# Attention: the first addition of each block's sum of probabilities moves to VectorE, and one tile's sum from TensorE to GpSimd

## Chip, cores, metric

One core of a Trainium2 chip runs the whole program. The metric is the device time of one execution in microseconds; the time before is the median of three runs.

## What is computed

A transformer layer with a scale and an offset from a condition, then a second layer of running averages. Only the attention of the first layer matters here:

```python
q = h @ wq / jnp.sqrt(jnp.asarray(d, h.dtype))      # 16 heads of 32, b = 2, l = 2048
...
q = rotary_pos_emb(q)
k = rotary_pos_emb(k)
logits = jnp.einsum('bhik,bhjk->bhij', q, k)
a = jax.nn.softmax(logits, axis=-1)
y = jnp.einsum('bhij,bhjv->bhiv', a, v)
```

The softmax is taken apart: `exp(logit - max)` for each query and key, the sum of these over the keys (`l` in the kernel), and the product with `v` that is divided by the sum later on.

## The kernel before

The attention stage works through 8 units (4 groups of 4 heads, 2 sequences), each of 4 blocks of 512 queries, each block of 16 steps. A step is one tile `k` of 128 keys for the 4 heads of the group. `attend` writes out, engine by engine, what is done in each of the 512 steps; an engine takes its instructions in that order, and semaphores tie the engines together.

- **TensorE** (lines 811 to 830): for each head a score matmul (L735, keys by queries, into one of three PSUM tiles `sT`) and, for a block 19 steps ahead, a matmul for the maxima (L763, into one of three PSUM tiles `mx`). Then the product of the step before with `v` (L787). Where the tile of the step before is in `PE_SUMS` (8 and 14), matmuls with a matrix of ones add its probabilities over the keys (L798). At step 5 of the next block (`LAST_AT`) one more such sum, over `acc`, ends the block's sum (L806).
- **VectorE**: `maxima` reduces each `mx` tile (L845); TensorE may fill an `mx` tile again when its reduction is done. Twice per 16 steps there is a small extra operation (L851, L860).
- **ScalarE**: `exps` takes the exponential of each score tile (L891) into `probs`, a ring of `PR` = 8 tiles of 4 heads x 512 queries. A tile of the ring is written again 8 steps later, and only when whoever sums it has read it (`added`, `summed`). Once per block it copies the finished values (L898, `o_sb`) and the finished sum (L904, `l_sb`).
- **GpSimd**: `add_pair` issues a DMA that adds tile `k` + 1 onto tile `k` for `k` in `PAIRS` (L924). `add_round` adds one tile, or one such pair, onto `acc` (`prob_sums`), head by head, four additions per round (L942). `POOL_ROUNDS` lists for each round the step at which it is issued, counted from the block's start, and the tile it reads: (18, 12) is the pair 12 and 13, added in step 2 of the next block. The first round starts `acc` from tile 2 (`POOL_FIRST`) and pair 0 (tiles 0 and 1).
- **SyncE** loads the next unit's keys, values and queries during a unit and stores the results.

So of the 16 tiles TensorE sums two (8 and 14), and the other 14 go through `acc`: ten in pairs by DMA, and tiles 2, 5, 11 and 15 directly. The last block of the stage has lists of its own (`LAST_SUMS`, `LAST_ROUNDS`). The maxima are made by `AHEAD` = 19 steps earlier than their use, so the last 19 steps of the stage have none.

Of the kernel before, what the change touches and what calls it, by code (L numbers as in the profile page):

```python
# [9 lines left out]
ALU = mybir.AluOpType  # L10
# [6 lines left out]
G = P // KD  # L17
# [5 lines left out]
TT = TB // P  # L23
# [10 lines left out]
PR = 8  # L34
PE_SUMS = (8, 14)
PAIRS = (0, 3, 6, 9, 12)
POOL_FIRST = 2
POOL_ROUNDS = ((5, 0), (7, 5), (9, 3), (11, 6), (12, 11), (14, 9), (16, 15), (18, 12))
# [5 lines left out]
LAST_AT = 5  # L44
# [528 lines left out]
def attend(nc, c, a, s, t, ps):  # L573
# [25 lines left out]
    def added(w, h):  # L599


        k = w % LT - (w % LT - 1 in PAIRS)
        r = 0 if k == POOL_FIRST else [x for _, x in POOL_ROUNDS].index(k)
        return w // LT * POOL_ADDS + G * r + h + 1
# [13 lines left out]
    with nc.Block() as block:  # L618
# [106 lines left out]
        def _(pe):  # L725
# [65 lines left out]
            def sums(w):  # L791

                n, k = w // LT, w % LT
                if k == PE_SUMS[0] and n:
                    pe.wait_ge(s["l_kept"], n)
                pe.wait_ge(s["exp"], G * (w + 1))
                for h in range(G):
                    mm = nc.tensor.matmul(l_ps[h * KD:(h + 1) * KD, :], c["ones"][:, 0:KD], t["p"][:, w % PR, h, :],  # L798
                                          start=(k == PE_SUMS[0]), stop=False)
                mm.then_inc(s["psum"], 1)  # L800
# [35 lines left out]
        def _(dve):  # L836
# [25 lines left out]

            for at, st in enumerate(steps):
                for i in range(TT if st["job"] else 0):
                    maxima(st, i)
# [12 lines left out]
        def _(act):  # L878
            def exps(at, heads):
                for h in heads:  # L880
                    if at >= PR:

                        v = at - PR
                        if not by_pe(v):
                            act.wait_ge(s["acc_done"], added(v, h))
                        elif h == 0:
                            act.wait_ge(s["psum"], summed(v))
                        if h == 0:
                            act.wait_ge(s["pv"], v + 1)
# [26 lines left out]
        def _(pool):  # L916
# [9 lines left out]
            def add_round(n, r):  # L926
# [5 lines left out]
                for h in range(G):  # L932
                    pool.wait_ge(s["exp"], w * G + h + 1)
                    x = t["acc"][:, n % 2, h, :]
                    if r == 0:
                        if n >= 2:
                            pool.wait_ge(s["sum_done"], n - 1)
                        first = t["p"][:, POOL_FIRST % PR, h, :]
                    else:
                        pool.wait_ge(s["acc_done"], n * POOL_ADDS + G * (r - 1) + h + 1)  # L940
                        first = x
                    nc.gpsimd.tensor_tensor(x, first, t["p"][:, w % PR, h, :], ALU.add).then_inc(s["acc_done"], 1)  # L942
# [16 lines left out]
def attention(nc, c, a, t):  # L959

    with ExitStack() as ctx:
        def sb(name, shape, dt=F32):
# [8 lines left out]
                 "score exp pv psum acc_done paired0 paired1 l_in recip rl_stored sum_done o_kept l_kept y_stored l_stored "  # L971
# [1015 lines left out]
```

## Time and profile before

| what | value |
|---|---|
| median of three runs | 3648.7 us (3648.08 to 3656.93) |
| the profiled execution: its time | 3653.45 us |
| the profiled execution: its span | 3651.7 us |
| granted TensorE clock, mean over the span | 0.973 |
| attention stage within the span | 396 to 2098 us |
| TensorE, VectorE, ScalarE, GpSimd busy | 95%, 56%, 41%, 57% |

The span is the time from the first to the last instruction in the trace, and all stretches below are counted from its start. "Busy" of an engine is the time in which an instruction ran on it. A granted clock of 1.00 is 2.4 GHz. Neighbouring instructions of one engine overlap a little in the records, so the distance between starts is shorter than a duration. In a timeline, instructions of one kind that follow each other are merged into a row with their number (x4); the bracket at the end says how long the engine was idle before, and what ended it. GpSimd is called POOL there, VectorE DVE, ScalarE ACT, TensorE PE, and its weight loads PEld.

### The profile page before, as it was taken

What the parts mean: (1) busy time and instruction counts of PE and PEld (TensorE: products, weight loads), DVE (VectorE), ACT (ScalarE), POOL (GpSimd) and SP (SyncE); (2) the same over time, 40 slices, a digit from 0 to 9 for tenths busy, and PEclk for the clock granted to TensorE, in tenths of its full rate; (3) what the DMA queues carried; (4) which work ended last, traced back from release to release, by engine and by line L of the source; (5) the groups of instructions that cost most, each with busy time, mean ns of one, the idle gap of its engine ahead of it and who ended that gap; (6) DMA issues with size and microseconds to landing.
All of it is one profiled execution on the core that took longest, in us unless ns stands there. A gap on an engine that the chain in (4) does not pass through costs nothing. (4 is left out here: it accounts for less than half of the span.)

```text
span 3651.7 us, 47181 instructions
## 1 busy us (share of the span) xinstructions
PE 3451.7 (95%) x16672; PEld 2252.2 (62%) x16672; DVE 2051.3 (56%) x3299; ACT 1515.4 (41%) x2791; POOL 2095.9 (57%) x1663
## 2 busy tenths in 40 slices
PE   7999899999999999999999969999999986999997
PEld 5777445454554545455455348888888864777776
DVE  5776677777777777777777244222222213444443
ACT  2332366666666666666666622111111112211121
POOL 3654388887878888798888712222222213545453
PEclk9999899999999999999999979999999997999999
DMA  4555676868677786877765543222222114212221
GB/s 170 183 172 196 119 145 126 154 132 146 132 139 151 127 145 131 153 140 132 151 128 107 105 149 97 65 63 74 74 71 68 57 41 143 80 59 82 75 75 38
DMA packets 176739, 419.34 MB, mean 115 GB/s; under 512 B 15382, under 2 KB 62998, under 8 KB 151670
## 3 DMA queue, kind: packets, MB, share of 16 engines
q1 hardware_dynamic: 153606, 249.59, 25.9%
q0 software_dynamic: 22896, 166.73, 23.7%
q8 instruction: 132, 2.16, 0.3%
q14 instruction: 105, 0.86, 0.1%
HBM read 162.25 MB, written 87.03 MB: 68 GB/s over the span
## 5 line engine op out<-in xcount | busy, mean ns | idle before, releaser
L845 DVE TENSOR_REDUCE part_max<-ps_att 128x1 f32<-128x512 f32 x1972 | 1227.9, 684 | 400.3 <-PE ps_att L763 399.9
L891 ACT ACTIVATE probs<-ps_att 128x512 f32<-128x512 f32 x2048 | 1062.4, 602 | 545.1 <-PE ps_att L735 469.8
L942 POOL TENSOR_TENSOR prob_sums<-prob_sums,probs 128x512 f32<-128x512 f32 x884 | 1146.9, 1562 | 61.8 <-DMA probs<-probs 61.8
L787 PE MATMUL ps_att<-probs,v_tok 128*32 128x512 f32 x4096 | 550.7, 610 | 0.0
L1433 POOL TENSOR_TENSOR ff_g_lo<-ff_g,ff_g_hi 128x512 fp32r<-128x512 f32 x128 | 165.1, 1290 | 551.6 <-DVE ff_g_hi L1394 551.6
L735 PE MATMUL ps_att<-q_stack,k_first 97*128 97x512 f32 x768 | 328.0, 427 | 14.1 <-ACT probs L891 14.0
L735 PE MATMUL ps_att<-q_stack,k_stack 97*128 97x512 f32 x768 | 321.4, 427 | 10.6 <-ACT probs L891 10.0
L1302 ACT ACTIVATE ff_g<-ps_ff 128x512 f32<-128x512 f32 x128 | 76.8, 600 | 579.6 <-PE ps_ff L1186 579.6
L763 PE MATMUL ps_att<-k_first,q_stack 96*128 96x512 f32 x756 | 304.6, 403 | 7.3 <-DMA q_stack<-qk 7.3
L763 PE MATMUL ps_att<-k_stack,q_stack 96*128 96x512 f32 x768 | 303.7, 395 | 0.0
L735 PEld LDWEIGHTS ps_att<-q_stack,k_first 97*128 97x128 f32 x768 | 146.5, 191 | 199.4 <-ACT probs L891 141.3
L735 PEld LDWEIGHTS ps_att<-q_stack,k_stack 97*128 97x128 f32 x768 | 143.7, 189 | 199.1 <-ACT probs L891 146.6
L924 POOL DMA_DIRECT2D probs<-probs x159 | 152.3, 958 | 178.1 <-PE ps_att L787 161.8
L1876 POOL TENSOR_TENSOR av_gated_lo<-av_full,av_gated_hi 128x512 fp32r<-128x512 f32 x64 | 93.3, 1457 | 267.3 <-ACT av_gated_hi L1729 267.3
L1394 DVE CAST ff_g_hi<-ff_g 128x512 fp32r<-128x512 f32 x128 | 55.8, 436 | 299.6 <-ACT ff_g L1302 299.6
L942 POOL TENSOR_TENSOR prob_sums<-probs 128x512 f32<-128x512 f32 x128 | 165.1, 1434 | 52.6 <-DMA probs<-probs 50.0
L787 PEld LDWEIGHTS ps_att<-probs,v_tok 128*32 128x32 f32 x4096 | 80.9, 108 | 184.0 <-ACT probs L891 174.4
L553 POOL TENSOR_TENSOR rotated<-rot_a,rot_b 128x512 f32<-128x512 f32 x64 | 89.8, 1403 | 153.9 <-DVE rot_b L394 150.2
L763 PEld LDWEIGHTS ps_att<-k_first,q_stack 96*128 96x128 f32 x756 | 146.3, 194 | 34.3 <-DMA q_stack<-qk 7.8
L763 PEld LDWEIGHTS ps_att<-k_stack,q_stack 96*128 96x128 f32 x768 | 145.7, 190 | 26.3
L1729 ACT ACTIVATE av_gated_hi<-av_full 128x512 fp32r<-128x512 f32 x64 | 40.6, 634 | 262.8 <-DVE av_full L1837 262.8
L1186 PE MATMUL ps_ff<-ff_h_hi,w_hi 128*128 128x512 f32 x512 | 143.3, 402 | 0.7 <-ACT ff_h_hi L1314 0.7
(202 smaller groups left out, 5705.0 us busy)
## 6 DMA issues: line engine op xcount, KB each, us to landing
probs<-probs POOLq DMA_DIRECT2D x159, 1024.0 KB, 8.7
q_stack<-qk SPq DMA_DIRECT2D x144, 128.0 KB, 7.2
qk<-rot_hi SPq DMA_DIRECT2D x64, 256.0 KB, 6.5
qk<-rot_lo SPq DMA_DIRECT2D x64, 256.0 KB, 2.4
av_gate_rows<-gate SPq DMA_DIRECT2D x64, 256.0 KB
k_stack<-qk SPq DMA_DIRECT2D x24, 512.0 KB, 11.0
k_first<-qk SPq DMA_DIRECT2D x18, 512.0 KB, 10.8
x_in_sb<-in_x SPq DMA_DIRECT2D x8, 1024.0 KB, 6.7
```

The costliest lines, as they stand in the source:

```text
L553: nc.gpsimd.tensor_tensor(rot[:, u % 2, :], ra[:, u % 2, :], rb[:, u % 2, :], ALU.add)\
L735: nc.tensor.matmul(sT[u % 3], kS[b][0:S3 + 1, h, k * P:(k + 1) * P], q_rows(n)[0:S3 + 1, h, :], start=True, stop=True)\
L763: nc.tensor.matmul(mx[mx_uses % 3], q_rows(n)[0:S3, h, q * P:(q + 1) * P], kS[b][0:S3, h, k * TB:(k + 1) * TB], start=True, stop=True).the ...
L787: mm = nc.tensor.matmul(o_ps[rows, :], t["v"][:, steps[w]["b"], k, rows], t["p"][:, w % PR, h, :], start=(k == 0), stop=(k == LT - 1))
L845: nc.vector.tensor_reduce(t["pm"][:, r, k:k + 1], mx[mx_uses % 3], AX.X, ALU.max)\
L891: nc.scalar.activation(t["p"][:, at % PR, h, :], sT[(at * G + h) % 3], ACT.Exp)\
L924: nc.gpsimd.dma_start(t["p"][:, w % PR], t["p"][:, (w + 1) % PR], accum_op=ALU.add).then_inc(sem, 16)
L942: nc.gpsimd.tensor_tensor(x, first, t["p"][:, w % PR, h, :], ALU.add).then_inc(s["acc_done"], 1)
L1186: mm = nc.tensor.matmul(ps[:, 4 + u % 2, :], w[:, f, m * P:(m + 1) * P], h[:, f, :], start=(i == 0 and f == 0), stop=(i == 2 and f == DC - 1))
L1302: nc.scalar.activation(gf[:], ps[:, 4 + u % 2, :], ACT.Gelu_apprx_tanh).then_inc(s["g"], 1)
L1433: nc.gpsimd.tensor_tensor(gl[:, u % 2, :], gf[:], gh[:, u % 2, :].bitcast(F32), ALU.subtract)\
L1876: nc.gpsimd.tensor_tensor(al[:, v % 2, :], af[:, v % 2, :], ah[:, v % 2, :].bitcast(F32), ALU.subtract).then_inc(s["a_lo"], 1)
```

## The change

`PE_SUMS` becomes (8,), so TensorE sums tile 8 alone. VectorE begins each block's sum: `begin_sum` adds tile 2 to pair 0 for one head and writes `acc`, and `DVE_AT` puts the four heads into steps 6 and 7, in each behind the maxima 1 and 3 of the four. A semaphore of its own, `acc_begun`, counts them; ScalarE waits for it before it overwrites tiles 0, 1 and 2, and GpSimd's first round (tile 5) before it adds. VectorE now waits for pair 0's transfer. GpSimd's first round goes, and a round for tile 14 comes at offset 20, which is step 4 of the next block. The last sum and the copy of it move two steps on (`LAST_AT` 5 to 7).

```diff
--- before.py
+++ after.py
@@ -32,16 +32,17 @@
 EPS2 = 1e-6
 EPS_ATT = 1e-30
 PR = 8
-PE_SUMS = (8, 14)
+PE_SUMS = (8,)
 PAIRS = (0, 3, 6, 9, 12)
-POOL_FIRST = 2
-POOL_ROUNDS = ((5, 0), (7, 5), (9, 3), (11, 6), (12, 11), (14, 9), (16, 15), (18, 12))
+DVE_SUMS = (0, 2)
+DVE_AT = ((6, 1, 0), (6, 3, 1), (7, 1, 2), (7, 3, 3))
+POOL_ROUNDS = ((7, 5), (9, 3), (11, 6), (12, 11), (14, 9), (16, 15), (18, 12), (20, 14))
 POOL_ADDS = G * len(POOL_ROUNDS)
 LAST_SUMS = (8, 11, 12, 13, 14, 15)
 LAST_ROUNDS = tuple(x for x in POOL_ROUNDS if x[1] not in LAST_SUMS)
 K_AT = (2, 6, 10, 14, 18, 22)
 V_AT = (26, 30)
-LAST_AT = 5
+LAST_AT = 7
 STEPS = NB * LT
 UNITS = NG * B
 JOBS = G * TT
@@ -600,8 +601,10 @@
 
 
         k = w % LT - (w % LT - 1 in PAIRS)
-        r = 0 if k == POOL_FIRST else [x for _, x in POOL_ROUNDS].index(k)
-        return w // LT * POOL_ADDS + G * r + h + 1
+        if k in DVE_SUMS:
+            return s["acc_begun"], w // LT * G + h + 1
+        r = [x for _, x in POOL_ROUNDS].index(k)
+        return s["acc_done"], w // LT * POOL_ADDS + G * r + h + 1
 
     def pair_sem(n, k):
         m = n * len(PAIRS) + PAIRS.index(k)
@@ -791,12 +794,13 @@
             def sums(w):
 
                 n, k = w // LT, w % LT
-                if k == PE_SUMS[0] and n:
+                opening = k == shares(n)[0][0]
+                if opening and n:
                     pe.wait_ge(s["l_kept"], n)
                 pe.wait_ge(s["exp"], G * (w + 1))
                 for h in range(G):
                     mm = nc.tensor.matmul(l_ps[h * KD:(h + 1) * KD, :], c["ones"][:, 0:KD], t["p"][:, w % PR, h, :],
-                                          start=(k == PE_SUMS[0]), stop=False)
+                                          start=opening, stop=False)
                 mm.then_inc(s["psum"], 1)
 
             def last_sums(n):
@@ -860,9 +864,26 @@
                 nc.vector.tensor_copy(t["mT"][:, e % 2, :], mx[mx_uses % 3][0:JOBS, 0:P]).then_inc(s["mx_free"], 1)
                 mx_uses += 1
 
+            def begin_sum(n, h):
+
+
+                first, second = DVE_SUMS
+                if h == 0:
+                    sem, value = pair_sem(n, first)
+                    dve.wait_ge(sem, value)
+                    if n >= 2:
+                        dve.wait_ge(s["sum_done"], n - 1)
+                dve.wait_ge(s["exp"], (n * LT + second) * G + h + 1)
+                nc.vector.tensor_tensor(t["acc"][:, n % 2, h, :], t["p"][:, first % PR, h, :], t["p"][:, second % PR, h, :],
+                                        ALU.add).then_inc(s["acc_begun"], 1)
+
             for at, st in enumerate(steps):
-                for i in range(TT if st["job"] else 0):
-                    maxima(st, i)
+                for i in range(TT):
+                    if st["job"]:
+                        maxima(st, i)
+                    for k, behind, h in DVE_AT:
+                        if (k, behind) == (st["k"], i):
+                            begin_sum(at // LT, h)
                 if ending is not None:
                     keep_maxima(ending)
                     ending = None
@@ -882,7 +903,8 @@
 
                         v = at - PR
                         if not by_pe(v):
-                            act.wait_ge(s["acc_done"], added(v, h))
+                            sem, value = added(v, h)
+                            act.wait_ge(sem, value)
                         elif h == 0:
                             act.wait_ge(s["psum"], summed(v))
                         if h == 0:
@@ -933,13 +955,10 @@
                     pool.wait_ge(s["exp"], w * G + h + 1)
                     x = t["acc"][:, n % 2, h, :]
                     if r == 0:
-                        if n >= 2:
-                            pool.wait_ge(s["sum_done"], n - 1)
-                        first = t["p"][:, POOL_FIRST % PR, h, :]
+                        pool.wait_ge(s["acc_begun"], n * G + h + 1)
                     else:
                         pool.wait_ge(s["acc_done"], n * POOL_ADDS + G * (r - 1) + h + 1)
-                        first = x
-                    nc.gpsimd.tensor_tensor(x, first, t["p"][:, w % PR, h, :], ALU.add).then_inc(s["acc_done"], 1)
+                    nc.gpsimd.tensor_tensor(x, x, t["p"][:, w % PR, h, :], ALU.add).then_inc(s["acc_done"], 1)
 
             nc.gpsimd.memset(t["k1"][S3:S3 + 1].bitcast(F32), 1.0).then_inc(s["ones_set"], 1)
             pool.wait_ge(s["ones_set"], 1)
@@ -968,7 +987,7 @@
             o=sb("o_sb", [P, TB]), l=sb("l_sb", [P, TB]))
         ps = ctx.enter_context(nc.psum_tensor("ps_att", [P, 8, 512], F32))
         names = ("q_in0 q_in1 q_in2 q_in3 q_first1 q_first2 v_first k_in v_in mx_full mx_free neg_max max_set0 max_set1 "
-                 "score exp pv psum acc_done paired0 paired1 l_in recip rl_stored sum_done o_kept l_kept y_stored l_stored "
+                 "score exp pv psum acc_begun acc_done paired0 paired1 l_in recip rl_stored sum_done o_kept l_kept y_stored l_stored "
                  "ones_set")
         s = phase(nc, ctx, " ".join("at_" + n for n in names.split()))
         s = {n[3:]: v for n, v in s.items()}
```

VectorE, in the attention stage, from a block's maxima on (before):

```order
L845 TENSOR_REDUCE part_max<-ps_att 128x1 x4
L860 CAST max_turned<-ps_att 16x128
L845 TENSOR_REDUCE part_max<-ps_att 128x1 x60
L851 TENSOR_REDUCE neg_max_sb<-part_max 128x16
L845 TENSOR_REDUCE part_max<-ps_att 128x1 x4
```

And in the changed kernel, the same place:

```order
L849 TENSOR_REDUCE part_max<-ps_att 128x1 x4
L864 CAST max_turned<-ps_att 16x128
L849 TENSOR_REDUCE part_max<-ps_att 128x1 x34
L877 TENSOR_TENSOR prob_sums<-probs 128x512
L849 TENSOR_REDUCE part_max<-ps_att 128x1 x2
L877 TENSOR_TENSOR prob_sums<-probs 128x512
L849 TENSOR_REDUCE part_max<-ps_att 128x1 x2
L877 TENSOR_TENSOR prob_sums<-probs 128x512
L849 TENSOR_REDUCE part_max<-ps_att 128x1 x2
L877 TENSOR_TENSOR prob_sums<-probs 128x512
L849 TENSOR_REDUCE part_max<-ps_att 128x1 x20
L855 TENSOR_REDUCE neg_max_sb<-part_max 128x16
```

The row of 60 maxima is cut open: four additions stand in it, two maxima apart.

GpSimd, from the issue of pair 0 (step 2) to that of pair 9 (step 11), before:

```order
L924 DMA probs<-probs 128x2048
L942 TENSOR_TENSOR prob_sums<-prob_sums,probs 128x512 x4
L924 DMA probs<-probs 128x2048
L942 TENSOR_TENSOR prob_sums<-probs 128x512 x4
L942 TENSOR_TENSOR prob_sums<-prob_sums,probs 128x512 x4
L924 DMA probs<-probs 128x2048
L942 TENSOR_TENSOR prob_sums<-prob_sums,probs 128x512 x4
L924 DMA probs<-probs 128x2048
```

In the changed kernel:

```order
L946 DMA probs<-probs 128x2048
L961 TENSOR_TENSOR prob_sums<-prob_sums,probs 128x512 x8
L946 DMA probs<-probs 128x2048
L961 TENSOR_TENSOR prob_sums<-prob_sums,probs 128x512 x4
L946 DMA probs<-probs 128x2048
L961 TENSOR_TENSOR prob_sums<-prob_sums,probs 128x512 x4
L946 DMA probs<-probs 128x2048
```

Between the issue of pair 0 and that of pair 3 stand eight additions instead of four, and between pair 3 and pair 6 four instead of eight.

## Rows read from the trace of the kernel before

**Rows 1.** The page: span, then each engine's busy time, share and instructions.
```profile
span 3651.7 us, 47181 instructions
...
PE 3451.7 (95%) x16672; PEld 2252.2 (62%) x16672; DVE 2051.3 (56%) x3299; ACT 1515.4 (41%) x2791; POOL 2095.9 (57%) x1663
```

**Rows 2.** Busy time by stretch, attention; columns PE, PEld, DVE, ACT, POOL, TensorE clock, DMA.
```profile
928.00:1034.00 106.00, 106.00 (x578) 53.77 (x576) 82.53 (x136) 70.12 (x136) 88.52 (x74) 1.00 0.67 130
396.00:2098.00 1702.00, 1666.45 (x8947) 832.17 (x8947) 1246.68 (x2035) 1094.97 (x2112) 1404.72 (x1172) 0.99 0.74 136
```

**Rows 3.** Groups of instructions by line: busy us, mean ns, idle before.
```profile
L845 DVE TENSOR_REDUCE part_max<-ps_att 128x1 f32<-128x512 f32 x1972 | 1227.9, 684 | 400.3 <-PE ps_att L763 399.9
L942 POOL TENSOR_TENSOR prob_sums<-prob_sums,probs 128x512 f32<-128x512 f32 x884 | 1146.9, 1562 | 61.8 <-DMA probs<-probs 61.8
...
L798 PE MATMUL ps_att<-probs,ones 128*32 128x512 f32 x544 | 71.7, 599 | 0.0
...
L1367 DVE TENSOR_TENSOR ff_zT_lo<-ff_zT,ff_zT_hi 128x512 fp32r<-128x512 f32 x32 | 22.2, 693 | 1.1
```

**Rows 4.** Timeline of TensorE, step 9 of a block (start us, us).
```profile
1027.24 0.50 PE L735 MATMUL ps_att<-q_stack,k_first 97*128 97x512 f32 x1
...
1030.23 1.04 PE L798 MATMUL ps_att<-probs,ones 128*32 128x512 f32 x8
1031.20 0.51 PE L735 MATMUL ps_att<-q_stack,k_first 97*128 97x512 f32 x1
```

**Rows 5.** Timeline of all engines, one step without sums, microsecond 1004.68 onwards.
```profile
1004.68 0.50 PE L735 MATMUL ps_att<-q_stack,k_first 97*128 97x512 f32 x1
...
1005.45 2.48 DVE L845 TENSOR_REDUCE part_max<-ps_att 128x1 f32<-128x512 f32 x4 [0.61 <-PE ps_att L763]
...
1006.22 0.19 PEld L763 LDWEIGHTS ps_att<-k_stack,q_first 96*128 96x128 f32 x1
1006.45 0.40 PE L763 MATMUL ps_att<-k_stack,q_first 96*128 96x512 f32 x1
...
1007.78 0.50 PE L735 MATMUL ps_att<-q_stack,k_first 97*128 97x512 f32 x1
```

**Rows 6.** Timeline of GpSimd, steps 2 to 5 of the same block.
```profile
1005.33 0.88 POOL L924 DMA_DIRECT2D probs<-probs  x1 [0.78 <-PE ps_att L787]
1005.94 5.29 POOL L942 TENSOR_TENSOR prob_sums<-prob_sums,probs 128x512 f32<-128x512 f32 x4
1014.63 0.88 POOL L924 DMA_DIRECT2D probs<-probs  x1 [3.40 <-PE ps_att L787]
1015.24 5.29 POOL L942 TENSOR_TENSOR prob_sums<-probs 128x512 f32<-128x512 f32 x4
```

**Rows 7.** Timeline of VectorE and GpSimd, a VectorE subtraction in the last stage.
```profile
3253.45 1.30 POOL L1876 TENSOR_TENSOR av_gated_lo<-av_full,av_gated_hi 128x512 fp32r<-128x512 f32 x1 [2.61 <-ACT av_gated_hi L1729]
...
3253.92 1.37 DVE L1737 TENSOR_TENSOR av_zT_lo<-av_zT,av_zT_hi 128x512 fp32r<-128x512 f32 x1 [1.22 <-ACT av_zT_hi L1675]
```

**Rows 8.** Timeline of ScalarE, copies of finished values; one per block.
```profile
888.55 0.60 ACT L898 ACTIVATE o_sb<-ps_att 128x512 f32<-128x512 f32 x1 [0.52 <-PE ps_att L787]
...
950.08 0.60 ACT L898 ACTIVATE o_sb<-ps_att 128x512 f32<-128x512 f32 x1 [0.52 <-PE ps_att L787]
...
1001.71 0.60 ACT L898 ACTIVATE o_sb<-ps_att 128x512 f32<-128x512 f32 x1 [0.56 <-PE ps_att L787]
```

**Rows 9.** Timeline of GpSimd (pair 0 in three blocks), then of ScalarE (first block).
```profile
432.43 4.93 POOL L942 TENSOR_TENSOR prob_sums<-probs 128x512 f32<-128x512 f32 x4 [10.52 <-DMA probs<-probs]
...
490.83 4.95 POOL L942 TENSOR_TENSOR prob_sums<-probs 128x512 f32<-128x512 f32 x4 [9.52 <-DMA probs<-probs]
...
699.53 5.01 POOL L942 TENSOR_TENSOR prob_sums<-probs 128x512 f32<-128x512 f32 x4 [3.52 <-DMA probs<-probs]
...
423.97 2.06 ACT L891 ACTIVATE probs<-ps_att 128x512 f32<-128x512 f32 x4 [1.01 <-PE ps_att L735]
...
433.72 0.60 ACT L891 ACTIVATE probs<-ps_att 128x512 f32<-128x512 f32 x1 [4.61 <-POOL prob_sums L942]
```

## The prediction

> **What bounds the kernel now.** I began with the page [rows 1]: over the whole span TensorE is busy 95% of the time and no other engine 60%. But the change touches only the attention stage, so next came the busy time by stretch. In a quiet stretch of two blocks [rows 2] TensorE is busy for all of 106 us at a granted clock of 1.00 (2.4 GHz), VectorE for 78%, ScalarE for 66% and GpSimd for 84%. Then the timelines, to see that this is a bound and not an average. A step without sums runs from one first score to the next in 3.10 us, 1004.68 to 1007.78 [rows 5]; step 9, with the sum of tile 8, takes 3.96 us, 1027.24 to 1031.20, with the sums at 1030.23 inside it [rows 4]. So a sum costs 0.86 us of TensorE time, and it goes into the period undiminished. Sixteen steps and three sums (two tiles, and the last sum over `acc`) make 16 x 3.10 + 3 x 0.86 = 52.2 us, and a quiet block takes 1001.71 - 950.08 = 51.6 us [rows 8]. TensorE sets the pace of most blocks. The exception is a block in each unit where the loads of the next unit's keys delay the pair transfers: 950.08 - 888.55 = 61.5 us is the longest [rows 8]. I count seven such blocks with 2 to 10 us each over the quiet period, some 34 us together.
>
> GpSimd does 32 additions and five DMA issues for a block. Read by the mean duration, 32 x 1.562 = 50.0 us [rows 3], it would be full. But four of them in a row take 5.29 us with the last one counted whole [rows 6], so they start (5.29 - 1.56) / 3 = 1.24 us apart: 32 x 1.24 + 5 x 0.6 = 43 us, and the 84% of [rows 2] says the same. The Trainium skill, Perfetto Trace Analysis, section GPSIMD Engine Instruction, warns that a GpSimd span is unreliable and that spacing of starts is the thing to read; the rows agree, and by the spans a sum would come out at no gain at all.
>
> **TensorE: one sum less.** The sums of tile 14 go in 31 blocks (the last keeps its own list). The group has 544 instructions, eight for a tile, so 68 tiles [rows 3], of which 31 go: 31 x 0.86 = **-26.7 us** if nothing else fills the place. The last sum moves from step 5 to step 7; it costs the same there.
>
> **GpSimd: no more and no less.** The round that began the sum goes, a round for tile 14 at offset 20 comes: 32 additions as before. The order changes, though. In step 2 it issues pair 0 (1005.33), then adds tile 12's round (1005.94), and is free until it issues pair 3 at 1014.63, after waiting 3.40 us [rows 6]. The new round of 4 x 1.24 = 5.0 us goes into this hole, and pair 3 leaves about 1.6 us later, at 1016.2 on that clock. Its reader is the round at offset 9, four steps or 12.4 us on. Tile 14's buffer is wanted by ScalarE in step 6, one step after the round's end. The last sum, now in step 7, waits for it too, but it is over by then. I cost the round at nothing; the cover is the 3.4 us hole and 8 us of slack per block. Without that cover the reader of tile 14's buffer, ScalarE, would stand for what is missing.
>
> **VectorE: four additions of 128x512.** Two go into step 6 and two into step 7, each behind the second and the fourth maximum. Their price alone is that of the subtraction of two SBUF tiles in the second stage, 0.693 us [rows 3]; in a row they start about 0.60 us apart as the maxima do, (2.48 - 0.68) / 3 [rows 5]. What is queued behind them is the maxima, and for those TensorE waits: with three PSUM tiles, the fourth maximum's matmul of a step may begin only when the first one has been reduced. Count from the first score of step 6, with the offsets of [rows 5]. The first maximum is reduced from +0.77, the fourth matmul is at +1.77 and its weights at +1.54; the reduction ends at +1.45, so the slack is between 0.09 and 0.32 us, and I take 0.15.
> Step 6: maxima at 0.77 and 1.37, addition at 1.97 (ends 2.66), maxima at 2.57 and 3.17, second addition ready at 3.77. GpSimd adds to the first head's result from about 2.74 to 4.04 (1.30 us as in [rows 7]). That collides. In [rows 7] a VectorE subtraction of two SBUF tiles that began 0.47 us into a GpSimd addition lasted 1.37 us, and ended 0.54 us after the GpSimd one. So the second addition here ends at 4.04 + 0.54 = 4.58 and not at 4.46, and step 7's first maximum begins at 4.49 where it began at 3.87: 0.62 us late. Less the slack, TensorE stands for **0.47 us** in step 7. In step 7 the same happens, but this step now has the last sum in it and gives VectorE 0.86 us to catch up: its fourth addition ends about 8.5, step 8's first maximum is ready at 3.10 + 0.47 + 3.96 + 0.77 = 8.3, late by about the slack. No second stall. With no collision the lateness is 0.50 and the stall 0.18 to 0.41; with the slack at its least and the collision it is 0.53. Over 31 blocks: 31 x 0.47 = **+14.6 us**, bounds 5.6 and 16.4.
> The rule behind this is in the Trainium skill, SBUF - State Buffer, section Who interferes with whom: a VectorE instruction with two SBUF inputs and a GpSimd instruction that reads SBUF share one pair of ports, and the second to start is blocked until the first is over. It speaks against the change, and the rows agree with it.
>
> **The wait for pair 0 moves to VectorE.** GpSimd used to wait for that transfer, in time that it had; now VectorE waits at step 6, with the maxima behind it. In quiet blocks it has landed: the round on it began at 1015.24 behind pair 3 without a wait [rows 6]. In the first two blocks it has not: GpSimd got pair 0 at 432.43 and 490.83 [rows 9]. Step 6 of the first block started its exponentials at 423.97, so the addition would be due near 425.4 and is held 7 us, and TensorE with it from step 7's second maximum. The kernel before stood there too, but in step 8, from 431 on, and only until 433.72 [rows 9], then at GpSimd's pace. The difference is about 2.5 us in the first block and 2 in the second: **+4.5 us**, bounds 0 and 9. In the seven slow blocks GpSimd is rid of a wait and issues its pairs up to 1.1 us sooner: **-1 us**, bounds 0 and -7.
>
> **The sum.** -26.7 + 14.6 + 4.5 - 1.0 = -8.6 us. The profiled execution has a span of 3651.7 and a time of 3653.45 us; the median of the three runs is 4.75 us under the latter. I set the change against the median: 3648.7 - 8.6 = **3640 us**. The bounds of the terms together give -28 to +1.
>
> **Rivals.**
> (a) The additions are hidden wholly: the slack is larger than the rows let me see, and nothing of the stall is left. For it: VectorE is idle 0.61 us in each step [rows 5], 9.8 us a block, against 2.5 us of additions. Against it: the offsets. Time: 3648.7 - 26.7 = 3622. Chance 0.17.
> (b) Slower: every VectorE addition meets a GpSimd addition just begun and takes about 1.29 us of VectorE's time. Step 6 then holds 4 x 0.60 + 2 x 1.29 = 4.98 us of VectorE's work against a period of 3.10; the lateness of 1.88 gives a stall of 1.7, and step 7 adds 1.0 more after its sum. 2.7 - 0.86 = 1.8 us a block, 57 us: 3706. It decides against the change from a stall of 0.86 on, which is a lateness of 1.0 us, one collision of full length and no more. For it: GpSimd's new round ends only 2 us before the first addition is due, and one late transfer puts it on top. Against it: GpSimd's next round waits for each of VectorE's additions, head by head, so the two engines take turns. In full it is improbable, in part less so. Chance 0.15. By the rule of the Trainium skill named above this is what follows wherever GpSimd starts first.
> (c) Pair 0 comes late for VectorE in the blocks with loads as well, 2.3 us in each of the seven: 16 us, and 3640 + 16 = 3656. For it: the first two blocks. Against it: the longest later wait of GpSimd for pair 0 was 3.52 us, until 699.53 [rows 9], and VectorE asks one step later. Chance 0.14.
> (d) TensorE is not the bound after all and GpSimd or the transfers keep the period at 51.6: no change, 3649. The undiminished 0.86 us in [rows 4] speaks against it. Chance 0.04.
> My forecast, TensorE's gain less a short stall in step 7, has the other 0.50, with a range of its own from 3632 to 3650.
>
> **How the numbers follow.** What a measurement of this kernel can tell from no change is about 0.3%, 10.9 us. Faster than 3637.8: all of (a), 0.17, and 0.21 of the forecast's 0.50: 0.38. Slower than 3659.6: 0.13 of (b) and 0.05 of (c): 0.18. Within: the rest, 0.44. For the range I leave out the far part of (b) and the edge of (a): 3621 to 3661.
>
> **What would show it.** In the profile after: the sums group at 296 instructions instead of 544; a quiet block at 51.6 - 0.4 = 51.2 us; VectorE's additions at a mean between 0.7 and 0.9 us; idle time of TensorE's weight load before the fourth maximum of step 7, put down to VectorE, some 15 us in all; step 8 without such a stall; GpSimd's additions still 1.24 us apart. A quiet block at 50.7 would prove (a), means over 1.2 us on VectorE (b), VectorE waiting for the pair transfers beyond the second block (c), an unchanged 51.6 without stalls on VectorE (d).

## The result, and the profile after

| | before | after |
|---|---|---|
| median of four runs each | 3648.4 us | 3700.4 us |
| ratio, 95% interval | | 1.0128 (1.0109 to 1.0147) |
| span of the profiled execution | 3651.7 us | 3697.7 us |
| attention: first and last copy of values | 466.6, 2096.7 us | 469.1, 2135.6 us |

The change makes the kernel 52 us slower, where the text above forecast 9 us faster and a range up to 3661. Of the 46 us between the two spans 39 lie in the attention stage, up to the last copy of values; the other 7 are in the stages behind it, which the change does not touch; from the last copy of values to the end took 1555 to 1561 us in the other kernels of this study, 1562 here. The page (the span, then busy time, share and instructions of each engine):

```profile
span 3697.7 us, 46937 instructions
...
PE 3449.1 (93%) x16424; PEld 2252.7 (61%) x16424; DVE 2141.7 (58%) x3427; ACT 1514.2 (41%) x2791; POOL 2093.3 (57%) x1659
```

The busy time by stretch; the first row has the same microseconds as the quiet stretch of before in [rows 2], but here a stop ends in it, so it is no longer a quiet one; the second is the stage, and the last three a stop that is read below:

```profile
928.00:1034.00 106.00, 103.64 (x539) 52.28 (x543) 86.22 (x141) 66.85 (x130) 88.45 (x74) 0.96 0.66 130
396.00:2150.00 1754.00, 1658.24 (x8699) 828.22 (x8699) 1341.79 (x2168) 1097.96 (x2118) 1401.88 (x1168) 0.97 0.73 133
704.00:708.00 4.00, 0.31 (x2) 0.00 (x0) 0.00 (x0) 1.05 (x2) 0.00 (x0) 0.99 1.10 145
708.00:712.00 4.00, 1.39 (x3) 1.16 (x4) 2.74 (x5) 0.07 (x1) 1.26 (x1) 0.50 1.03 205
716.00:720.00 4.00, 4.00 (x21) 2.35 (x22) 2.81 (x5) 3.02 (x6) 4.00 (x4) 1.00 0.43 86
```

The groups of instructions by line:

```profile
L961 POOL TENSOR_TENSOR prob_sums<-prob_sums,probs 128x512 f32<-128x512 f32 x1008 | 1303.8, 1594 | 214.5 <-DVE prob_sums L877 137.8 <-ACT probs L913 69.1 <-DMA probs<-probs 7.6
...
L766 PE MATMUL ps_att<-k_first,q_stack 96*128 96x512 f32 x756 | 308.2, 408 | 42.8 <-DVE part_max L849 35.3 <-DMA q_stack<-qk 7.5
...
L877 DVE TENSOR_TENSOR prob_sums<-probs 128x512 f32<-128x512 f32 x128 | 108.3, 848 | 69.8 <-DMA probs<-probs 69.8
...
L802 PE MATMUL ps_att<-probs,ones 128*32 128x512 f32 x296 | 38.5, 592 | 0.0
```

The edit did what it says. TensorE's sums are 296 instructions where they were 544 [rows 3], VectorE's additions are there at a mean of 0.85 us, GpSimd adds nearly as often as before (1008 for 884 + 128; the last block has a round less). New are the waits of TensorE's maxima matmul for VectorE (35.3 us in this group alone, where the same group had none before) and 69.8 us in which VectorE stood before its additions for the transfer of pair 0.

**A quiet block** goes as the working above has it. VectorE's timeline in steps 6 to 8:

```profile
1032.61 1.29 DVE L849 TENSOR_REDUCE part_max<-ps_att 128x1 f32<-128x512 f32 x2 [0.62 <-PE ps_att L766]
1033.82 0.68 DVE L877 TENSOR_TENSOR prob_sums<-probs 128x512 f32<-128x512 f32 x1
1034.42 1.28 DVE L849 TENSOR_REDUCE part_max<-ps_att 128x1 f32<-128x512 f32 x2
1035.62 0.87 DVE L877 TENSOR_TENSOR prob_sums<-probs 128x512 f32<-128x512 f32 x1
1036.41 1.27 DVE L849 TENSOR_REDUCE part_max<-ps_att 128x1 f32<-128x512 f32 x2
1037.61 0.84 DVE L877 TENSOR_TENSOR prob_sums<-probs 128x512 f32<-128x512 f32 x1
...
1039.57 0.85 DVE L877 TENSOR_TENSOR prob_sums<-probs 128x512 f32<-128x512 f32 x1
1040.34 2.47 DVE L849 TENSOR_REDUCE part_max<-ps_att 128x1 f32<-128x512 f32 x4
```

The first addition takes 0.68 us; the others 0.84 to 0.87, as they run into GpSimd's. TensorE in step 7 of the same block (its first score, its fourth score, its fourth maximum, then the first score of step 8):

```profile
1034.94 0.50 PE L738 MATMUL ps_att<-q_stack,k_first 97*128 97x512 f32 x1
...
1036.47 0.40 PE L738 MATMUL ps_att<-q_stack,k_first 97*128 97x512 f32 x1
1037.14 0.49 PE L766 MATMUL ps_att<-k_stack,q_first 96*128 96x512 f32 x1 [0.27 <-DVE part_max L849]
...
1039.42 0.50 PE L738 MATMUL ps_att<-q_stack,k_first 97*128 97x512 f32 x1
```

The fourth maximum's matmul has 0.27 us of idle time ahead of it, put down to VectorE, and step 7 lasts 1039.42 - 1034.94 = 4.48 us: 3.96 with the last sum, and a stop of 0.52. The reduction at 1040.34 follows on the last addition without a gap and TensorE does not wait for it. So this block loses 0.52 us of the 0.86 us (over the quiet blocks the median of step 7 is 4.51 us against 3.93 in tile14_only, which has the last sum there and no additions on VectorE: 0.58). Blocks that were 51.6 and 52.1 us are 51.5 and 51.8.

**A block with loads** does not go as worked out. VectorE in the second block of the program's second unit:

```profile
701.05 1.29 DVE L849 TENSOR_REDUCE part_max<-ps_att 128x1 f32<-128x512 f32 x2 [0.59 <-PE ps_att L766]
709.26 0.69 DVE L877 TENSOR_TENSOR prob_sums<-probs 128x512 f32<-128x512 f32 x1 [6.92 <-DMA probs<-probs]
709.87 1.28 DVE L849 TENSOR_REDUCE part_max<-ps_att 128x1 f32<-128x512 f32 x2
711.07 0.85 DVE L877 TENSOR_TENSOR prob_sums<-probs 128x512 f32<-128x512 f32 x1
```

It stood 6.92 us for the transfer of pair 0, with two maxima of step 6 and all that follows queued behind. TensorE's next maximum matmul came after that:

```profile
710.61 0.80 PE L766 MATMUL ps_att<-k_stack,q_stack 96*128 96x512 f32 x1 [6.31 <-DVE part_max L849]
```

TensorE did nothing from 704.3 to 710.6. The granted clock was 0.50 of full speed (1.2 GHz) between 708 and 712, in the stretches above; it had fallen during the stop, stayed there until after 714 and was back at 1.00 from 716 on. Two scores in between start 0.85 us apart instead of 0.47. Step 7 took 12.5 us, 8.0 more than in a quiet block, and the whole block 61.6 us where it had been 54.0. The DMA column says that the transfer engines were busy all the while (1.10 and 1.03). Pair 0 landed here 20.6 us after its issue at 688.6 (the line says count, duration of the issue, place):

```profile
L946 POOL DMA_DIRECT2D probs<-probs x1: 1012/1012/1012, 688.6 to 688.6; - x1
...
DMA to landing us min/median/max: 20.6/20.6/20.6
```

In the kernel before, the same transfer took 13.3 us:

```profile
L924 POOL DMA_DIRECT2D probs<-probs x1: 1067/1067/1067, 686.2 to 686.2; - x1
...
DMA to landing us min/median/max: 13.3/13.3/13.3
```

The copy of values, one per block, gives the length of each block. The kernels of the study are best told by it:

| kernel | median, us | ratio to before | first copy | mean of the seven second blocks of a unit | median of the other 21 |
|---|---|---|---|---|---|
| before | 3648.4 | 1 | 466.6 | 56.2 | 51.7 |
| the change | 3700.4 | 1.0128 | 469.1 | 60.5 | 51.8 |
| tile14_only | 3658.6 | 0.9996 (0.9972 to 1.0020) | 462.8 | 59.5 | 51.0 |
| vector_only | 3719.8 | 1.0169 (1.0118 to 1.0221) | 469.4 | 59.6 | 53.2 |
| begin_2_5 | 3654.3 | 1.0000 (0.9977 to 1.0024) | 466.0 | 56.2 | 51.8 |
| all_in_step7 | 3838.4 | 1.0491 (1.0445 to 1.0537) | 469.7 | 62.3 | 58.2 |
| after_loads | 3617.8 | 0.9893 (0.9870 to 0.9916) | 459.9 | 51.4 | 51.5 |
| before_loads | 3615.7 | 0.9887 (0.9866 to 0.9907) | 458.5 | 51.6 | 51.7 |
| after_two_loads | 3632.8 | 0.9945 (0.9923 to 0.9966) | 466.8 | 51.4 | 51.7 |
| tile14_loads | 3605.4 | 0.9859 (0.9840 to 0.9879) | 458.5 | 52.2 | 50.9 |
| tile14_loads_b | 3620.8 | 0.9906 (0.9882 to 0.9930) | 457.6 | 51.3 | 51.2 |
| tile14_loads_q | 3652.2 | 0.9988 (0.9976 to 0.9999) | 458.3 | 52.8 | 54.0 |

"Second block of a unit" is here the distance from the copy in the unit's second block to that in its third, in the profiled execution; the loads of the next unit's keys at steps 18 and 22 fall in it. The kernel before had medians of 3653 to 3658 us beside the experiments and not 3648.4, so the ratios count, not the differences of medians.

By the same copies the 39 us of the attention stage divide so: 2.5 before the first copy, 30.0 in the seven second blocks, 8.0 in the first blocks of the seven later units, and -1.6 in the rest. In three of those first blocks VectorE stood 1.4, 1.4 and 1.8 us for pair 0, and step 7 took 6.0, 7.6 and 8.1 us instead of 4.5: a short wait can cost more than its own length. VectorE's first addition and two of TensorE's matmuls in the second of the three:

```profile
868.22 0.69 DVE L877 TENSOR_TENSOR prob_sums<-probs 128x512 f32<-128x512 f32 x1 [1.38 <-DMA probs<-probs]
...
869.57 0.50 PE L766 MATMUL ps_att<-k_first,q_stack 96*128 96x512 f32 x1 [0.74 <-DVE part_max L849]
...
871.55 0.65 PE L766 MATMUL ps_att<-k_first,q_stack 96*128 96x512 f32 x1 [0.65 <-DVE part_max L849]
```

After these two stops of 0.7 us the granted clock was 0.50 in the stretch 872 to 874; in the first of the three blocks, from 650 to 656, it stayed at 1.00.

### The profile page after: what moved, and what is told of

It is laid out like the page before. It is cut to its first block and busy times, and to the rows that moved or that the text cites. A ratio compares the mean times of both kernels' runs of the same rounds, so it can differ in the third digit from the quotient of the medians.

```text
span 3697.7 us, 46937 instructions
## 1 busy us (share of the span) xinstructions
PE 3449.1 (93%) x16424; PEld 2252.7 (61%) x16424; DVE 2141.7 (58%) x3427; ACT 1514.2 (41%) x2791; POOL 2093.3 (57%) x1659
## 5 line engine op out<-in xcount | busy, mean ns | idle before, releaser
L961 POOL TENSOR_TENSOR prob_sums<-prob_sums,probs 128x512 f32<-128x512 f32 x1008 | 1303.8, 1594 | 214.5 <-DVE prob_sums L877 137.8
L766 PE MATMUL ps_att<-k_first,q_stack 96*128 96x512 f32 x756 | 308.2, 408 | 42.8 <-DVE part_max L849 35.3
L946 POOL DMA_DIRECT2D probs<-probs x159 | 160.3, 1008 | 117.4 <-PE ps_att L790 112.9
L877 DVE TENSOR_TENSOR prob_sums<-probs 128x512 f32<-128x512 f32 x128 | 108.3, 848 | 69.8 <-DMA probs<-probs 69.8
L1856 DVE TENSOR_TENSOR av_full<-ps_avg,av_gate_rows 128x512 f32<-128x512 f32 x64 | 44.2, 690 | 177.1 <-PE ps_avg L1642 139.7
```

The lines of the kernel that those rows point to most:

```text
L766: nc.tensor.matmul(mx[mx_uses % 3], q_rows(n)[0:S3, h, q * P:(q + 1) * P], kS[b][0:S3, h, k * TB:(k + 1) * TB], start=True, stop=True).the ...
L877: nc.vector.tensor_tensor(t["acc"][:, n % 2, h, :], t["p"][:, first % PR, h, :], t["p"][:, second % PR, h, :], ALU.add).then_inc(s["acc_be ...
L946: nc.gpsimd.dma_start(t["p"][:, w % PR], t["p"][:, (w + 1) % PR], accum_op=ALU.add).then_inc(sem, 16)
L961: nc.gpsimd.tensor_tensor(x, x, t["p"][:, w % PR, h, :], ALU.add).then_inc(s["acc_done"], 1)
```

## The experiments

My theory after the result, W: the loss is VectorE's wait for pair 0, which holds the maxima behind it and so TensorE. Its rivals: G, the added round of tile 14 makes GpSimd late; P, the two engines' additions hold each other up. In the edits below, lists are shortened with "...", and in the kernels with `PE_SUMS = (8,)` the line that opens a block's sum on TensorE is as in the change.

**tile14_only.** TensorE's part without VectorE's.

```diff
--- before
-PE_SUMS = (8, 14)
+PE_SUMS = (8,)
-POOL_ROUNDS = (..., (16, 15), (18, 12))
+POOL_ROUNDS = (..., (16, 15), (18, 12), (20, 14))
-LAST_AT = 5
+LAST_AT = 7
```

> Only TensorE's part of the change: tile 14 goes to GpSimd in a ninth round at offset 20, GpSimd still begins each block's sum from tile 2 and pair 0, VectorE adds nothing; GpSimd has 36 additions for a block, 36 x 1.24 + 3 = 47.6 us of a block of 51. Theory W (the loss is VectorE's wait for pair 0, which holds the maxima and so TensorE): the blocks with loads keep their 54 to 61 us or lose a little to the fuller GpSimd, quiet blocks come to 50.8 us, and the time is 3622 to 3640 us, faster than before. Theory G (the loss is the sum's later end and the added round of tile 14 on GpSimd, which delays the issue of pairs 3 and 6): slower than before, 3680 us or more.

Ratio 0.9996: neither theory's time. The quiet blocks came to 50.7 and 51.2 us, the whole 0.86 us less, with GpSimd at 101.45 of 106 us in the stretch of [rows 2]:

```profile
928.00:1034.00 106.00, 105.42 (x563) 53.30 (x562) 82.90 (x136) 70.45 (x136) 101.45 (x87) 1.00 0.63 130
```

But the second blocks took 59.5 us on the mean (57.5 to 65.3). There ScalarE stood for GpSimd at step 4, where it overwrites tile 12:

```profile
691.61 0.60 ACT L892 ACTIVATE probs<-ps_att 128x512 f32<-128x512 f32 x1 [7.02 <-POOL prob_sums L943]
```

Pair 12 had been issued at 673.1 and needed 17.2 us:

```profile
L925 POOL DMA_DIRECT2D probs<-probs x1: 812/812/812, 673.1 to 673.1; - x1
...
DMA to landing us min/median/max: 17.2/17.2/17.2
```

So a second thing is at work that has nothing to do with VectorE: in these blocks the transfers of pairs come late, and whoever has to wait for them can stop the whole. W was right that GpSimd can take the round; it had left out that the saved time is lost again at the next late transfer.

**vector_only.** VectorE's part alone.

```diff
--- the change
-PE_SUMS = (8,)
+PE_SUMS = (8, 14)
-POOL_ROUNDS = (..., (18, 12), (20, 14))
+POOL_ROUNDS = (..., (18, 12))
-LAST_AT = 7
+LAST_AT = 5
```

> Only VectorE's part of the change: it begins each block's sum with tile 2 and pair 0 as in the change, TensorE keeps the sums of tiles 8 and 14, GpSimd has seven rounds, the last sum stays at step 5. Theory W: all of the loss is here, some 6 us in each unit's second block and about 0.5 us in each quiet block, with no gain against it: 3700 to 3725 us. Theory G: with GpSimd freed of a round there is no loss beyond 31 stalls of 0.5 us: about 3665 us.

Ratio 1.0169, at the upper end of what W expected; G's is out. Quiet blocks lost 1.5 us, not 0.5. VectorE's timeline in steps 6 to 9, three of the additions and the maxima after them:

```profile
1039.39 0.68 DVE L877 TENSOR_TENSOR prob_sums<-probs 128x512 f32<-128x512 f32 x1
...
1041.19 0.86 DVE L877 TENSOR_TENSOR prob_sums<-probs 128x512 f32<-128x512 f32 x1
...
1045.14 0.85 DVE L877 TENSOR_TENSOR prob_sums<-probs 128x512 f32<-128x512 f32 x1
1045.91 2.47 DVE L849 TENSOR_REDUCE part_max<-ps_att 128x1 f32<-128x512 f32 x4
1048.85 2.48 DVE L849 TENSOR_REDUCE part_max<-ps_att 128x1 f32<-128x512 f32 x4 [0.46 <-PE ps_att L766]
```

The additions cost the same as in the change. But here step 7 has no last sum in it, VectorE is still behind in step 8 (the four maxima at 1045.91 follow the last addition at once) and TensorE stops twice: step 7 lasts 3.65 us and step 8 3.94 (medians of the quiet blocks), where a step without a sum lasts 3.07. That is the second stop that the prediction worked out as absent, and it is absent only because the last sum stands in step 7.

**begin_2_5.** VectorE adds tiles that no transfer touches.

```diff
--- the change
-DVE_SUMS = (0, 2)
+DVE_SUMS = (2, 5)
-POOL_ROUNDS = ((7, 5), ...)
+POOL_ROUNDS = ((7, 0), ...)
-                    sem, value = pair_sem(n, first)
-                    dve.wait_ge(sem, value)
```

> The change, but VectorE begins each sum with tiles 2 and 5, which no transfer touches, at the same four places; GpSimd's first round, at offset 7, adds pair 0. Same number of additions on each engine. Theory W: the stalls of 6 to 8 us in the blocks with loads shrink to those of the kernel before (2 to 10 us over a quiet block), quiet blocks lose another 0 to 0.5 us since ScalarE waits in step 8 for GpSimd's round on pair 0: 3640 to 3660 us. Theory P (the loss is the shared port between VectorE's and GpSimd's additions): as the change, 3695 to 3705 us.

Ratio 1.0000, in W's range; the second blocks are back at 56.2 us, quiet blocks as in the change. The additions are as many, stand at the same places and last as long (the median, 841 ns), and what VectorE stood for ahead of them has gone but for one case:

```profile
L875 DVE TENSOR_TENSOR prob_sums<-probs x128: 677/841/4005, 425.7 to 2066.9; 128x512 f32<-128x512 f32 x128
...
  ACT probs L911: 6.8, 1
```

The one case is in the last block, where no maxima stand behind it. This is the run that settles W against P: as many additions, each as long, no wait for the transfer, no loss against the kernel before. Pair 0 was late here as well, 20.5 to 21.8 us in the second blocks; GpSimd, which asked for it with its own additions behind, could bear most of it. ScalarE stood for GpSimd 2.1 to 3.4 us in each of them, and they are still 4.4 us over the others.

**all_in_step7.** The same additions one step closer together.

```diff
--- the change
-DVE_AT = ((6, 1, 0), (6, 3, 1), (7, 1, 2), (7, 3, 3))
+DVE_AT = ((7, 0, 0), (7, 1, 1), (7, 2, 2), (7, 3, 3))
```

> The change with all four of VectorE's additions in step 7, one behind each maximum, so that VectorE asks for pair 0 some 2.5 us later. Theory W: each of the seven or eight long waits is 2 to 2.5 us shorter, 15 to 20 us less in all; four additions in one step cost quiet blocks 0.5 to 1 us more than in the change, 12 to 25 us: 3690 to 3710 us, with the waits of VectorE for the transfer down from 8 us to 6 and quiet blocks at 52 to 52.5 us. Theory P: longer by more than that, as the additions and GpSimd's meet in one step: over 3715 us, and the waits for the transfer unchanged.

Ratio 1.0491, where the change has 1.0128: some 130 us more. The time is on P's side, with no upper end given; the waits for the transfer did shrink, from 69.8 to 46.1 us, as W said and P did not. But a quiet block took 58.2 us, where W had 52 to 52.5. Each addition but the first met one of GpSimd's in full, 1.46 us instead of 0.69; an addition, and the maximum after it:

```profile
1027.92 1.46 DVE L877 TENSOR_TENSOR prob_sums<-probs 128x512 f32<-128x512 f32 x1
1029.31 0.68 DVE L849 TENSOR_REDUCE part_max<-ps_att 128x1 f32<-128x512 f32 x1
```

TensorE waited for two maxima in step 8, 1.2 us each:

```profile
1032.02 0.50 PE L766 MATMUL ps_att<-k_first,q_stack 96*128 96x512 f32 x1 [1.22 <-DVE part_max L849]
...
1033.98 0.80 PE L766 MATMUL ps_att<-k_first,q_stack 96*128 96x512 f32 x1 [1.23 <-DVE part_max L849]
...
1036.57 0.80 PE L738 MATMUL ps_att<-q_stack,k_first 97*128 97x512 f32 x1
```

Step 8 lasted from 1029.26 to 1036.57, 7.3 us instead of 3.1: 2.45 for the two stops, most of the rest because the clock fell in the second of them. Step 9, from there to 1043.85, has no stop at all and took 7.3 us instead of 4.0:

```profile
1031.00:1035.00 4.00, 1.75 (x7) 0.79 (x11) 4.00 (x6) 1.19 (x2) 2.80 (x3) 0.82 0.01 2
1035.00:1039.00 4.00, 4.00 (x14) 1.95 (x7) 1.73 (x4) 1.20 (x2) 4.00 (x5) 0.50 0.81 162
```

This is P's mechanism and my rival (b), shown, in a kernel that provokes it; the change itself meets it only with 0.16 us for each addition but the first.

After these four the question was why the pairs come late. SyncE issues 512 KB of keys at steps 2, 6, 10, 14, 18 and 22 of each unit; pair 0 is issued in step 2 of each block, which is step 18 of the unit in the second block. D says those loads stand beside it on the transfer engines. O says it is GpSimd's own order, pair 0 behind pair 12.

**after_loads, before_loads.** The loads of keys elsewhere, in the change and in the kernel before.

```diff
-K_AT = (2, 6, 10, 14, 18, 22)
+K_AT = (6, 10, 14, 23, 37, 40)
```

> The change, with the six loads of the next unit's keys at steps 6, 10, 14, 23, 37 and 40 of a unit where they were at 2, 6, 10, 14, 18 and 22, so that none is issued between a block's steps 1 and 5, when pair 0 is on its way. Theory D (pair 0 comes late because those loads share the transfer engines with it, and VectorE's wait turns the lateness into a stop of TensorE): pair 0 lands within 13 us in each unit's second block, VectorE's waits go, these blocks fall from 61 to 52 or 54 us, and the time is 3625 to 3645 us, 55 to 75 us under the change. Theory O (the order of GpSimd's own transfers, pair 0 behind pair 12, makes it late): pair 0 still lands after 18 us or more and the time stays over 3685 us.

> The kernel before with the same other places for the loads of keys: the control. Its seven blocks with loads are 34 us over the quiet period together. Theory D: most of that goes, 3620 to 3635 us. Theory O: 3640 to 3657 us.

D, in both, and with more than it asked for: 3617.8 us is 7 us under the range given, 3615.7 us 4 us under. In the change the second blocks went from 60.5 to 51.4 us, and the ratio is 0.9893. Over the whole run VectorE stood for the transfer 10.9 us instead of 69.8:

```profile
L877 DVE TENSOR_TENSOR prob_sums<-probs x128: 679/844/3442, 425.6 to 2031.4; 128x512 f32<-128x512 f32 x128
...
  DMA probs<-probs: 10.9, 3
```

Of the 10.9 us 7.5 are in the last block of the stage, where no maxima stand behind VectorE (of the 69.8 us in the change 7.3).

The longest landing of a pair fell from 21.8 to 17.6 us, in the kernel before from 20.5 to 14.0. The first block is part of it: the first copy of values comes 8 to 9 us earlier in both. The two now have the same time (3617.8 and 3615.7 us, the intervals overlap): with the loads moved the change is worth nothing, not 52 us of loss and not the 9 us of gain that I forecast.

**after_two_loads.** Which of the six loads.

```diff
--- the change
-K_AT = (2, 6, 10, 14, 18, 22)
+K_AT = (2, 6, 10, 14, 37, 40)
```

> The change with only the last two loads of keys moved, from steps 18 and 22 to 37 and 40; the four at steps 2 to 14 stay. Theory D2 (the two loads beside pair 0 of a unit's second block make the long waits): those blocks fall from 61 to about 52 us, 55 to 60 us less in all, while the first block of the program (20 us for pair 0) and the blocks that begin a unit keep what they lose: 3635 to 3650 us. Theory D4 (the backlog is built up by all six loads together): the second blocks stay over 55 us and the time is over 3660 us.

D2: 51.4 us in the second blocks, all of it from the loads at steps 18 and 22. The ratio is 0.9945 and 3632.8 us is 2 us under the range given. What is left to after_loads is in the first block (466.8 against 459.9) and in the blocks at a unit's turn, which the expectation had too: four of them took 54.4 to 56.2 us, with a wait of VectorE for pair 0 of 1.2 to 2.3 us in each. The short waits cost more than their own length, as read above.

**tile14_loads.** Tile 14 to GpSimd, nothing on VectorE, the loads at the places of before_loads.

> Tile 14 to GpSimd, nothing on VectorE, and the loads of keys moved. Tile 14 alone took each quiet block from 51.6 to 50.8 us and gave it back in the unit's second block, 57.5 to 59.5 us. Theory D: with the transfers on time both gains stay, 26 us from TensorE's sums and 20 to 30 us from the blocks with loads: 3595 to 3615 us. Theory F (GpSimd with nine rounds is full, and what it gave back there was its own lateness): the second blocks stay over 56 us and the time over 3630 us.

Ratio 0.9859 (0.9840 to 0.9879), 3605.4 us: better than both kernels and, against before_loads at 0.9887, 0.3% better than moving the loads alone. The intervals of the ratios overlap, but the four runs of each, taken beside each other, do not (3601.9 to 3607.6 us against 3610.4 to 3618.4). The quiet blocks keep their 50.7 to 51.2 us, but the gain is 10 us and not the 26 that D had from TensorE's sums. Four of the seven second blocks still take 52.5 to 54.5 us, so F may have a share: with nine rounds GpSimd has little in hand, and a late pair 12 (13 us where a unit ends) is felt.

**tile14_loads_b, tile14_loads_q.** Two attempts at the rest.

```diff
--- tile14_loads
-K_AT = (6, 10, 14, 23, 37, 40)
+K_AT = (6, 10, 22, 36, 38, 40)        tile14_loads_b
-                    if w % LT == 1 and w > LT:
+                    if w % LT == 9 and w > LT:        tile14_loads_q
```

> Tile 14 to GpSimd, loads of keys at steps 6, 10, 22, 36, 38 and 40: none at step 14, where pair 12 is issued and lands after 13 us. If that load is what is left of the slow blocks (52.5 to 54.5 us), they come to 51 us and the time to 3595 to 3603 us; if not, it stays at 3605 us.

> The same, and the loads of the next unit's queries (six transfers each) at a block's step 9 where they were at step 1. Theory D: each such load also stood beside pair 0; another 0 to 10 us less than without it. Theory F: no difference.

Neither gained. In tile14_loads_b pair 12 landed after 9 to 10 us and the second blocks did get better (51.3 us), so the load at step 14 was what was left in them; but those after them, which now hold three loads in five steps, take 53 to 56 us, and one took 65: 3620.8 us. In tile14_loads_q pair 0 landed in 7 to 8 us in the second blocks, as D has it, but pairs 3 and 6, next to the moved loads, in 12 to 15 there: 3652.2 us. GpSimd's waits for transfers between 460 and 2000 us are 112 us in all where tile14_loads has 48, and ScalarE's for GpSimd 159 where it has 56. The load has to stand somewhere, and each pair has a reader; here moving it off one transfer moved it onto the next.

The block of 65 us in tile14_loads_b has another wait on top: a score matmul stood for the small transfer that brings the maxima into `q_stack`.

```profile
1189.80 0.73 PE L735 MATMUL ps_att<-q_stack,k_stack 97*128 97x512 f32 x1 [4.74 <-DMA q_stack<-max_turned]
```

Why this transfer was late in one block alone was not tested.

## Why the prediction was wrong

- **TensorE sets the pace, and a sum is worth 0.86 us.** Right. tile14_only took 0.86 us off every quiet block.
- **GpSimd: the round costs nothing.** Right in quiet blocks, with eight rounds and even with nine. The mean duration of 1.56 us per addition would have had it full; by the spacing of the starts it was not. The Trainium skill, Perfetto Trace Analysis, section GPSIMD Engine Instruction, calls such spans unreliable and goes by the spacing, and the run with nine rounds agrees: 36 additions at 1.56 us are 56 us, and its blocks took 51.
- **VectorE: one stop of 0.47 us, in step 7 alone.** Right in kind and place; 0.52 us in the block read above and 0.58 in the median, just over the upper bound of 0.53. The additions lasted 0.85 us where one of them had been worked out at 0.81. vector_only showed that the absence of the second stop hangs on the last sum standing in step 7, as the working had it. The lock of the ports, which the Trainium skill, SBUF — State Buffer, section Who interferes with whom, describes for a VectorE instruction with two SBUF inputs beside a GpSimd instruction that reads SBUF, fits what was seen in both sizes: 0.85 us when an addition runs into the end of GpSimd's, 1.46 us when it starts just behind it.
- **The wait for pair 0 moves to VectorE: +4.5 us, in the first two blocks.** This is the step that failed. The first two blocks cost 4.6 us together (2.5 until the first copy, 2.1 after), as said. But the same wait came back in the second block of the later units, where the sum charged nothing and only rival (c) had it: VectorE stood 6.0 to 8.1 us in each of six blocks. I had read GpSimd's wait there as 3.52 us at most and taken the landing and the time of VectorE's asking as they stood. Neither was fixed. In the kernel before, the pipeline stopped in those very blocks for pair 12, which made 61.5 us of one of them [rows 8], and during this stop pair 0 went on. ScalarE, in the kernel before, in step 4 of the block read above:

```profile
690.53 0.60 ACT L891 ACTIVATE probs<-ps_att 128x512 f32<-128x512 f32 x1 [2.38 <-POOL prob_sums L942]
```

In the change pair 12 came in time and nothing stopped there. Counted from the first score of the block, step 6 began after 21.6 us in the kernel before and pair 0 had landed after 23.2; in the change step 6 began after 18.4 and pair 0 landed after 27.4. So of the 7 us that VectorE stood, some 3 come from the stop that is gone, and 4 from the transfer itself, which took 20.6 us where it had taken 13.3. Rival (c) was the right one, but priced at 2.3 us for a block; four blocks of 54 us became 59 to 61.6, and only those that had been slow already changed little (61.5 to 60.9 and 58.5 to 60.8).
- **The clock.** No term had it. The stop of 6.3 us was followed by about 4 us of work at half clock, and two stops of 0.7 us in one step by some more, which the price of (c) would have needed.
- **Seven slow blocks gain 1 us from earlier issues.** Wrong in sign, by the same error: together they took 30.0 us more.
- **The net.** With the loads out of the way, the change and the kernel before differ by less than their intervals, where the terms other than the wait gave -13 us. Step by step, after_loads is 0.3 us shorter than before_loads in most blocks, as a quiet block should be. Two blocks, each the third of a unit, are 2.8 and 5.1 us longer; the other thirty are 4.5 us shorter together. In those two VectorE stood 1.3 and 2.1 us for pair 0, which took 14.9 and 15.8 us, and the granted clock was 0.70 in the stretch 944 to 948 and 0.50 in 1568 to 1572. So even with the loads moved it is the wait that takes the gain. The 4.5 us are less than the terms gave without it; 3.4 us of that are stops of 0.58 instead of 0.47 us in 31 blocks, the rest was not taken apart.
- **The bounds.** The bounds of the terms add up to -28 and -1, not to -28 and +1; the range given went further up than either.

What stays open: why pair 0 takes 20 us in the second block when it is issued 3 us earlier against the block than before. after_two_loads shows that the two loads of keys at steps 18 and 22 are needed for it. Where these stand and pair 0 left 6.8 us after the block's first score (the change, vector_only, begin_2_5), it took 17.0 to 21.8 us; where it left after 9.1 us or more (tile14_only, and the kernel before from the second unit on), 11.8 to 15.1; in the first unit of the kernel before it left after 8.9 us and took 18.5. That the earlier issue, closer behind the load of step 18, makes the difference is likely and was not tested; how the transfer engines share out between a load and a pair was not measured.

## What to carry to other kernels

When a wait is moved from one engine to another, its price is set by what stands behind it in the new engine's order, and by when the new engine asks; a wait that cost nothing on an engine with time in hand can stop the one that sets the pace. A landing time read from a trace holds only together with the stops and the times of issue in it: take away the stop during which a transfer went on, and the transfer is late; issue it at another time beside other transfers, and it takes another time. Look for the cause of a late transfer before arranging work around it. Here moving the six loads was worth 1.1%, one tile's sum moved from TensorE to GpSimd about 0.3% on top, and the whole change with VectorE's part nothing.

## What the runs showed of the hardware

- Two SBUF tiles of 128x512 float32 added by VectorE: 0.68 us alone, 0.84 to 0.87 us when the addition begins 0.3 us before the end of one of GpSimd's (the change), 1.44 to 1.46 us when it begins 0.36 us behind its start (all_in_step7).
- The granted clock: in a stop of 6.3 us (the change) it fell to 0.50, and it was back at 1.00 from 716 us, TensorE having gone on at 710.6. In all_in_step7 two stops of 1.2 us in step 8 went with 0.82 in the stretch 1031 to 1035, 0.50 from 1035 to 1043. In the change two stops of 0.7 us in one step went with 0.50 from 872 to 874. One stop of 0.5 us in a quiet block left it at 1.00.
- A transfer that adds one 1024 KB tile group onto another landed in 6.9 us at best and 8.6 us in the median (the change), and in 20 to 22 us in the second blocks, beside the 512 KB loads of steps 18 and 22.
